# A delta-rule stage regrouped: eight heads by 256 tokens for four heads by 512

## The reference

```
x = x + attention_a(norm(x))     # attention over the feature axis
x = x + experts(norm(x))         # six routed experts and a shared one
x = x + delta(norm(x))           # gated delta rule, 16 heads of 128
x = x + experts(norm(x))
```

```
q, k, v = silu(causal_conv4(x @ Wq | Wk | Wv) + bias)       # 4 taps along the tokens
g = -exp(A_log) * softplus(x @ Wfa @ Wfb + dt_bias);  beta = sigmoid(x @ Wb)
S = S * exp(g_t);  vd = (v_t - S^T k_t) * beta_t;  S = S + k_t vd^T;  o_t = S^T q_t
out = (o * rsqrt(mean(o*o)) * w * sigmoid(x @ Wga @ Wgb)) @ Wo
```

## Time and profile before

| | busy us | share |
|---|---|---|
| PE | 3474.6 | 94% |
| DVE | 1941.4 | 52% |
| ACT | 1427.4 | 38% |
| POOL | 125.0 | 3% |

### The profile page before, as it was taken

How to read it: one execution, slowest core, us unless ns; L and a number is a source line. 1 busy time by engine, 2 the same in 40 slices (tenths; PEclk the granted TensorE clock), 3 DMA queues, 4 the chain that set the end, 5 groups by cost and what they waited for, 6 DMA issues and landing times. The chain is left out here.

```text
span 3715.8 us, 86134 instructions
## 1 busy us (share of the span) xinstructions
PE 3474.6 (94%) x37416; PEld 1694.5 (46%) x37416; DVE 1941.4 (52%) x3334; ACT 1427.4 (38%) x3313; POOL 125.0 (3%) x457
## 2 busy tenths in 40 slices
PE   6979999996789999999999999999999759999999
PEld 4454444442344544444444444444444435444444
DVE  2131111113778897789878878887888431111111
ACT  1010000001466656666665666566656521000000
POOL 0000000000000000000000000000000000000000
PEclk9979999997989999999999999999999868999999
DMA  4011100003111111121111111111211042000000
GB/s 154 7 57 36 28 0 29 11 0 120 48 31 36 42 50 34 45 66 41 33 56 43 48 50 45 42 37 39 65 39 34 16 154 63 14 15 29 0 12 12
DMA packets 83725, 156.21 MB, mean 42 GB/s; under 512 B 8782, under 2 KB 33998, under 8 KB 79516
## 3 DMA queue, kind: packets, MB, share of 16 engines
q1 hardware_dynamic: 83356, 150.77, 12.3%
HBM read 133.71 MB, written 17.04 MB: 41 GB/s over the span
## 5 line engine op out<-in xcount | busy, mean ns | idle before, releaser
L1333 PE MATMUL psum<-dl_xt,dl_wqkv 128*128 128x512 f32 x1536 | 778.2, 624 | 10.4 <-DVE dl_qkv L977 10.0
L513 DVE SCALAR_TENSOR_TENSOR f_act_g<-psum,f_bup,f_act_g 128x512 f32<-128x512 f32 x96 | 72.1, 751 | 939.4 <-ACT f_act_g L468 939.4
L977 DVE SCALAR_TENSOR_TENSOR dl_qkv<-psum,dl_par,dl_qkv 128x511 f32<-128x511 f32 (+2 forms) x576 | 430.4, 747 | 14.0
L468 ACT ACTIVATE f_act_g<-psum,f_bgate 128x512 f32<-128x512 f32 x96 | 66.0, 687 | 923.1 <-PE psum L411 923.1
L1333 PEld LDWEIGHTS psum<-dl_xt,dl_wqkv 128*128 128x128 f32 x1536 | 257.4, 189 | 250.2 <-issue 212.5
L411 PE MATMUL psum<-xnt_sb,wup 128*128 128x512 f32 x768 | 345.2, 592 | 0.0
L407 PE MATMUL psum<-xnt_sb,wgate 128*128 128x512 f32 x768 | 345.2, 592 | 0.0
L429 PE MATMUL psum<-f_wdown,f_hidden 128*128 128x512 f32 x768 | 344.9, 592 | 0.0
L1340 PE MATMUL psum<-dl_wo,dl_sg 128*128 128x512 f32 x512 | 260.9, 623 | 2.9 <-DVE dl_qkv L977 2.5
L407 PEld LDWEIGHTS psum<-xnt_sb,wgate 128*128 128x128 f32 x768 | 145.9, 190 | 183.7 <-issue 183.7
L411 PEld LDWEIGHTS psum<-xnt_sb,wup 128*128 128x128 f32 x768 | 145.9, 190 | 183.7 <-issue 183.7
(11 more groups left out here) (192 smaller groups left out, 4618.1 us busy)
## 6 DMA issues: line engine op xcount, KB each, us to landing
dl_wqkv<-in_dw_qkv SPq DMA_DIRECT2D x192, 256.0 KB, 2.6
dl_wo<-in_dwo SPq DMA_DIRECT2D x16, 1024.0 KB, 5.2
f_weights_b<-f_weights_by_expert SPq DMA_DIRECT2D x48, 256.0 KB, 6.3
wgate<-in_wgate SPq DMA_DIRECT2D x2, 3072.0 KB, 18.6
wup<-in_wup SPq DMA_DIRECT2D x2, 3072.0 KB, 24.7
f_wdown<-in_wdown SPq DMA_DIRECT2D x2, 3072.0 KB, 13.6
x_sb<-in_x SPq DMA_DIRECT2D x4, 1024.0 KB, 9.3
x_after_experts<-x_sb SPq DMA_DIRECT2D x16, 256.0 KB, 2.0
```

Of the source, the lines that this page charges most:

```text
L977: tap_ = lambda dl: dve.scalar_tensor_tensor(y_[:, dl:TT], ps[:, bank, 0:TT - dl], par[:, h, 4 * a + 3 - dl:4 * a + 4 - dl], y_[:, dl:TT], ...
L1333: last = pe.matmul(ps[:, bank, :], wq[:, n % RING, m, :], xt[:, u // HG % 2, m, :], start=(m == 0), stop=(m == KC - 1))
```

## The change

A unit is now eight heads by 256 tokens (HU = 8, TT = 256). There are still 16 units, with eight slots each. A slot holds two groups of four heads (e = 0, 1), so that every piece of the recurrence has twice the matmuls and the chain is passed half as often. Tiles are laid out by chunk, `[g, j, t]`: group and chunk, head, token.

The further parts:
- A projection computes 256 tokens and three before them (HALO), 259 columns, from a tile `xt` that holds the three; the saved columns and their instructions go. There are 24 projections in a unit for 12, with weights loaded again for each block of tokens, in a ring of six buffers for four. `Wo` comes in quarters.
- `vrow` and `krow` use four transposes of 128 x 128 for sixteen small matmuls.
- Four long pieces stand in each slot, not split (`main_jobs`). All jobs share banks 4 to 7: each takes the bank whose last job ended longest ago (`place_jobs`).
- GpSimd takes the series (as three scalar and three two-input passes over 2048 elements), `near_zero`, `o_scale`, `decayed` and the early tokens' keys. `choose` and the sum behind it stand together on DVE.
- DVE's late tokens of a level are one instruction over 2048 elements for four over 512. Convolutions stand at fixed places, before or behind `add_state` (`done_before`, `done_behind`).

```diff
 HJ = 4
+HE = 2
+HU = HJ * HE
+HG = H // HU
 C = 32
-TT = 512
+TT = 256
 TN = T // TT
-NG = TT // C
+RB = TT // P
+HALO = 3
+CH = TT // C
+NG = HE * CH
 HB = C // 2
 LEVELS = 5
 KEPS = 1e-6
 UNITS = TN * HG
-SLOTS = NG
-RING = 4
+SLOTS = CH
+PROJ = 3 * HU
+RING = 6
+JOB_BANKS = (4, 5, 6, 7)
...
+def main_jobs(k, sl):
+
+    if sl in (3, 4):
+        jobs = [("rows", k - 1, i, q) for q in (2 * sl - 6, 2 * sl - 5) for i in range(RB)]
     else:
...
+        unit, first = {0: (k + 1, 8), 1: (k + 1, 12), 2: (k + 1, 16), 5: (k + 1, 20), 6: (k + 2, 0), 7: (k + 2, 4)}[sl]
+        jobs = [("proj", unit, first + n, 0) for n in range(4)]
+    return [(j[:3], j[3]) for j in jobs if 0 <= j[1] < UNITS]
...
+    table = {(0, "long"): [("vrow", k, 1)], (0, "inner"): [("vrow", k, 2)], (0, "split"): [("vrow", k, 3)],
+             (1, "inner"): [("gate", p, 0), ("gate", p, 1)], (1, "split"): [("gate", p, 2)], (1, "end"): [("gate", p, 3)],
+             (2, "long"): [("turn", p, 0), ("turn", p, 1)], (2, "inner"): [("turn", p, 2)], (2, "split"): [("turn", p, 3)],
+             (3, "states"): [("level", w, 0)], (3, "long"): [("level", w, 1)], (3, "end"): [("level", w, 2)],
+             (4, "states"): [("sums", w, 0)], (4, "long"): [("level", w, 3)], (4, "end"): [("level", w, 4)],
+             (5, "long"): [("level", w, 5)],
+             (6, "long"): [("krow", w, 0), ("dec", w2, 0)], (6, "inner"): [("krow", w, 1), ("dec", w2, 1)],
+             (6, "split"): [("dec", w2, 2)], (6, "end"): [("dec", w2, 3)],
+             (7, "states"): [("cross", w, 0)], (7, "long"): [("krow", w, 2)], (7, "inner"): [("krow", w, 3), ("corner", w, 0)],
+             (7, "end"): [("vrow", w, 0)]}
+    once = {(1, "end"): ("beta", w, 0), (3, "split"): ("ga", w, 0), (4, "split"): ("fa", w2, 0)}.get((sl, at))
...
+    last = {job: n for n, job in enumerate(order)}
+    ends, used, place = {b: -1 for b in JOB_BANKS}, {b: 0 for b in JOB_BANKS}, {}
+    for job in order:
+        if job not in place:
+            bank = min(JOB_BANKS, key=lambda b: ends[b])
+            place[job] = (bank, used[bank])
+            used[bank] += 1
+            ends[bank] = last[job]
...
+                def series(u):
+                    pool.wait_ge(s["softplus_exp"], u + 1)
+                    if u > 0:
+                        pool.wait_ge(s["softplus_sum"], u)
+                    for n, c in enumerate((1.0 / 3.0, -0.5, 1.0)):
+                        if n == 0:
+                            pool.tensor_scalar(poly[:, :], all_w, -0.25, c, ALU.mult, ALU.add).then_inc(s["series"], 1)
+                        else:
+                            pool.wait_ge(s["series"], 6 * u + 2 * n)
+                            pool.tensor_scalar(poly[:, :], poly[:, :], c, None, ALU.add).then_inc(s["series"], 1)
+                        pool.wait_ge(s["series"], 6 * u + 2 * n + 1)
+                        pool.tensor_tensor(poly[:, :], poly[:, :], all_w, ALU.mult).then_inc(s["series"], 1)
...
+                def early_keys(u, lv):
+                    m = 1 << (lv - 1)
...
+                    pool.tensor_tensor(kk_[:, :, 0, :], kk_[:, :, 0, :], dv[:, :, 1, 0:1].broadcast_to([P, HU * TT // (2 * m), m]),
+                                       ALU.mult).then_inc(s["early_keys"], 1)
...
+                    if prep:
+                        near_zero(w)
+                    if post:
+                        o_scale(p)
+                    if prep:
+                        decayed(w, QQ)
+                        decayed(w, KK)
+                        for lv in range(1, LEVELS + 1):
+                            early_keys(w, lv)
+                        solve(w)
+                    if ahead:
+                        series(w2)
...
+                def convolve(u, i):
+                    a, n = (QQ, KK, VV)[i // HU], i % HU
+                    h, bank = head(u, n), bank_of("proj", u, i)
+                    y_ = one_head(qkv[:, a], n)
+                    tap_ = lambda dl: dve.scalar_tensor_tensor(y_, chunks(ps[:, bank, HALO - dl:HALO - dl + TT]),
+                                                               par[:, h, 4 * a + 3 - dl:4 * a + 4 - dl], y_, ALU.mult, ALU.add)
+                    dve.wait_ge(s["tapped"], PROJ * u + i + 1)
+                    step(tap_(1))
+                    step(tap_(2))
+                    tap_(3).then_inc(read[bank], 1)
...
                 def choose(u):
                     ln, mask = flat(kq(u)[:, 0]), flat(kq(u)[:, 1])
-                    o.wait(mark[("near", u)])
-                    dve.wait_ge(s["series_done"], u + 1)
+                    dve.wait_ge(s["near_ready"], u + 1)
+                    dve.wait_ge(s["series"], 6 * u + 6)
                     dve.wait_ge(s["softplus_ln"], u + 1)
                     dve.tensor_copy(waited[:, 0:1], cst[:, K_ONE:K_ONE + 1])
...
+                def late_tokens(u, lv):
+                    m = 1 << (lv - 1)
+                    nb = HU * TT // (2 * m)
+                    dv = flat(dec[:]).rearrange("p (n r m) -> p n r m", r=2, m=m)
+                    late = kq(u).rearrange("p a g j t -> p a (g j t)").rearrange("p a (n r m) -> p a n r m", r=2, m=m)[:, :, :, 1, :]
+                    wait_full(dve, "level", u, lv)
+                    if lv > 1:
+                        dve.wait_ge(s["left"], LEVELS * u + lv - 1)
+                    dve.tensor_tensor(late, late, dv[:, :, 0, 0:1].unsqueeze(1).broadcast_to([P, 2, nb, m]),
                                       ALU.mult).then_inc(s["late"], 1)
...
+                    done_before = {0: [(w, 7), (w, 8), (w, 9)], 1: [(w, 11), (w, 12), (w, 13)], 2: [(w, 15), (w, 16), (w, 17)],
+                                   3: [(w, 19)], 4: [], 5: [(w, 20)], 6: [(w, 22), (w, 23), (w2, 0), (w2, 1)],
+                                   7: [(w2, 3), (w2, 4), (w2, 5)]}
+                    done_behind = {0: [(w, 10)], 1: [(w, 14)], 2: [(w, 18)], 3: [], 4: [], 5: [(w, 21)], 6: [(w2, 2)], 7: [(w2, 6)]}
...
+                        if sl == 2 and post:
+                            o_factor(p)
+                        if sl == 3 and post:
+                            gated(p, 2)
+                            gated(p, 3)
+                        if sl == 3 and prep:
+                            level_take(w, 0)
+                        if sl == 4 and prep:
+                            late_tokens(w, 2)
+                            level_take(w, 2)
+                            norm_rows(w)
+                        if sl == 5 and post:
+                            for n in range(RB):
+                                add_rows(p, n)
+                        if sl == 5 and prep:
+                            late_tokens(w, 4)
+                            level_take(w, 4)
+                        if sl == 7 and prep:
...
+                        convolutions(done_before, sl)
+                        if sl in (3, 4, 5) and prep:
+                            late_tokens(w, 2 * sl - 5)
 
                         if run:
                             add_state(k, sl)
...
+                        if sl == 5 and prep:
+                            whole_decay(w)
+                        if sl in (3, 4, 5) and prep:
+                            level_take(w, 2 * sl - 5)
+                        if sl == 1 and prep:
+                            choose(w)
+                        if sl == 4 and prep:
+                            turn_beta(w)
+                            norm_tables(w)
+                        if sl == 5 and prep:
+                            blocks_out(w)
+                        convolutions(done_behind, sl)
+                        if sl == 2 and post:
+                            gated(p, 0)
+                            gated(p, 1)
+                        if sl == 6 and prep:
                             blocks_in(w)
...
+                def by_rows(bank, src, n):
                     for m in range(4):
-                        for j in range(HJ):
-                            last = pe.matmul(ps[part(j), bank, P * m:P * m + P], chunk(src, g0 + m)[:, j, :], ident,
-                                             start=True, stop=True)
+                        g = CH * (m // 2) + 2 * n + m % 2
+                        last = pe.transpose(ps[:, bank, P * m:P * m + P], src[:, g].rearrange("p j t -> p (j t)"), ident)
                     return last
```

807 lines of the change are left out of this document (347 added, 460 removed).

## The result

The changed kernel takes 4037.08 us (median of four runs, 4031.73 to 4044.24) against 3720.62 for the kernel before: a ratio of 1.0855, with a 95% interval of 1.0831 to 1.0879. It is slower by 8.5%; the forecast was 3712 with a range up to 3815. The profiled execution has a span of 4031.5 us against 3715.8, so 315.7 us are to be found.

The account below looks back on a forecast made before the run. The prediction took TensorE, busy 94% of the span, as the bound. It summed 3717.97 + 26 (fifteen units) - 10 (start-up) - 20 (last unit) - 3 (what follows) = 3711, stated as 3712 us, range 3590 to 3815.

Parts of the forecast that it names:

- TensorE's work: TensorE's busy time in a unit at full clock: to fall from 121.3 to 111.9 us.
- the fourth turn: Slot 2: the fourth turn takes the first's bank, which VectorE's gated(p, 0) reads late; TensorE idle 4.3 us.
- level 0: TensorE's level 0 waits for VectorE's gated(p, 2): 1.0 us a unit.
- slot 6: Projection 1 needs a bank whose convolution (21) stands behind blocks_out at slot 5's end: a wait of 2.9 us.
- The wait of 2.0 at projection 16: Slots 1 and 2: projection 16 wants bank 7 at 16.0 us, free at 18.0 behind choose and a convolution.
- The last unit: Unit with nothing to prepare, a bare chain of eight passes: 56 us for 73.7, -20 with the shorter tail.
- The sum of the waits, 10.9 + 0.6: TensorE's new waits in a unit: 10.9 us from the named places and 0.6 for small ones.
- Rival C: GpSimd's series late, holding choose and the gates in slot 1 by 4 us a unit: 3772 us, chance 0.21.
- rival D: GpSimd and VectorE hinder each other, the series late by about 10 us a unit: 3862 us, chance 0.07.
- The part on levels: TensorE's levels, less broken up than before: 0.7 us less work a unit.
- The clock, 3.4: After slot 2's 4.3 us idle TensorE runs at half rate in most units: 3.4 us each, between 0 and 6.
- Start-up, -10: Before the first recurrence: half the tokens in a block, first norms, levels and tables sooner: -10 us (-20 to 0).

Follow-up runs that it names:

- both orders: Changed kernel with two operations, plus VectorE's gated(p, 0), gated(p, 1) ahead of add_state in slot 2 and convolution 21 ahead of blocks_out in slot 5: 3854.68 us.
- two operations: Changed kernel with an idle second operation (times 1.0) in GpSimd's three scalar passes that had one, near_zero's comparison included: 3934.48 us.
- the series on a sliver: Changed kernel with each GpSimd pass of the series on 16 of 2048 columns, and near_zero whole with two operations: 3903.76 us.
- runs with added waits: Kernel before, TensorE waiting behind solve_u of slot 5 in each unit for GpSimd's zero fills: ten fills 3801.71 us, five fills 3758.6 us.

## Why the prediction was wrong

**What held.** TensorE's work: 111.8 us for 111.9, so the weight loads stayed hidden, by an estimated 4 ns each. Three of the named waits: the fourth turn 3.7 us a unit (4.3), level 0 1.0 (1.0), slot 6 3.3 (2.9); the first and the last went in the run with both orders, though what stood just behind them then waited. The wait of 2.0 at projection 16 did not come, for projection 15 had already waited longer; once the gates are in time it shows in five of eleven units, up to 2.1 us. The last unit is 67.8 us for 73.7, where 56 was forecast; with all behind it, the gain is 14.0 and not 23.

**The sum of the waits, 10.9 + 0.6, is the step that failed.** It is 24.9. Two terms stood in it at nothing:
- GpSimd. I bounded a scalar pass between 1.8 and 3.9 us and took 2.9; it takes 5.4 to 5.5. The upper bound came from a two-input pass, on the thought that one input can't cost more. Rival C named the place and the limit (late from 3.3 us a pass). That the gates' 4.1 us are just its 4 is luck: its 4 belongs to passes of 3.9 us, and by its rule, one us a unit for each us late, an end 17.1 us into slot 1 for 7.6 would have cost 9.5. The run with two operations gave back 6.5 us a unit, 3.1 of them the clock's. That a small VectorE instruction stands until GpSimd's pass ends (rival D) was real and smaller than its 10: 1.3 us a unit for the series and at most 3.3 for the early keys. VectorE was to fall to 90 us a unit and is busy for 1073.77 / 11 = 97.6; its five decays of a level alone (L1100) take 1.87 us each beside GpSimd's passes and 0.72 without them.
- Pauses for instructions: 6.0 us a unit. The part on levels priced only their work, unbroken for broken up, as a gain of 0.7 a unit. What the halves had covered was not in any row of before, since there it never showed.

Of the rest, some 3 us are further waits for convolutions, most of them under 1.2 us, which a timetable with sums of 12 us and an error of 2 cannot see.

**The clock, 3.4.** It is 10.2. I gave it to one wait, the only one longer than that of the row that I had. The runs with added waits show that waits of 1.9 us cost it too, and in the eleven units of the changed kernel the clock fell to 0.50 fifty-five times, five times a unit.

**Start-up, -10.** It is +31.7. The chain of the first unit is bare: TensorE waited 20.0 us at one projection whose bank VectorE would read behind `choose`, and that waited for the 32 us of GpSimd. With the series on a sliver the first recurrence comes at 1063.73 for 1082.64. The rest of the loss, 12.8 us, was not taken apart; the table of waits puts 12.4 us of this stretch on TensorE's waits for GpSimd's `decayed` and early keys and 8.1 on instructions.

**Slips in the sums.** 3711 and 2.8 make 3714, not 3712. The 1.92 us are four records, which is two matmuls and not four; the halo then costs 0.5 us a unit by the same rows, not 0.6. Both are small beside the loss.

So the forecast's direction hung on waits and clock that were priced at 14.9 us a unit and are 35.1. No rival was near: C's 3772 and D's 3862 each added one cause to a forecast that lacked three.

## What to carry to other kernels

When an engine is busy for 97% of a unit, a change that saves 8% of its work has to be judged by the waits that it adds, and in the two runs with added waits each cost 1.4 times its length, for the clock. Twice the work in half as many slots, on four banks shared by all, leaves little between a job and its next user. Banks of their own for short and long jobs, as before, might help; no run here tests it. Bursts of tiny matmuls want long matmuls between them, as in the kernel before; to cut them in halves in this order removed a quarter of the pauses and lost more to the banks. Before a pass is given to an idle engine, time that very form of it there, and look at what the other engine does meanwhile.

## What the hardware did that I had not expected

- GpSimd, passes with one input over 2048 columns: multiply and add by constants 1.90 us, add alone 5.50, add and multiply 2.04; comparison alone 5.37, comparison and multiply 7.10.
- A GpSimd pass over two operands in SBUF holds up a VectorE pass over two operands in SBUF until it ends, and an addition of 5.37 us with one operand until 1.7 us before it ends (166 ns became 2.05 us on average and 4.5 at most). The convolutions, with an operand in PSUM, are not held up (482 ns with and without the series). The Trainium skill, "Advanced Engine Details and Errata", section "VectorE Performance Modes", says that VectorE's second port to SBUF is shared with GpSimd, so that they block each other; the rows agree for two operands in SBUF.
- TensorE pauses 1 to 4 us at a time for its own instructions, behind bursts of 128 matmul records of 16 to 32 columns, and goes on 1.15 to 1.65 us after a block of 16 KB of them has arrived (29 of 30 pauses).
